# Graph attention plus graph convolution, 64 graphs on one core: key products in two halves, their shared weight tile reloaded in halves, and the key sums taken from the split weights

## The reference, cut to what matters

```python
# x: (64, 256, 512), adj: (64, 256, 256), all float32; LN is a layer norm without gain
h = maximum(LN(x), 0)
query = h @ Wq.T + bq; keyt = h @ Wk.T + bk; value = h @ Wv.T + bv
weight = adj * exp(query @ keyt.T)
weight = weight / sum(weight, axis=2, keepdims=True)
x = x + weight @ value
h = maximum(LN(x), 0)
agg = (adj @ h) / maximum(sum(adj, -1, keepdims=True), 1e-6)
x = x + relu(concatenate([h, agg], 2) @ W.T)
```

## Time and profile before

| | us |
|---|---|
| median of 3 runs | 1933.32 (1931.07 to 1945.87) |
| the profiled execution, its own time | 1942.48 |
| its span | 1940.4 |
| PE busy in it | 1892.7 (98%) |
| DVE busy | 1579.6 (81%) |
| POOL busy | 1103.0 (57%) |
| ACT busy | 862.4 (44%) |
| DMA share of q1 | 57.2% of 16 engines |

### The profile page before, as it was taken

The page is one execution under the profiler, slowest core; times in us unless marked ns, Lnnn a source line. Parts: engine busy times, 40 slices in busy tenths (PEclk is TensorE's granted clock), DMA queues, the critical chain, the costliest instruction groups (busy, mean ns, idle before and its releaser), DMA issues.

```text
span 1940.4 us, 29261 instructions
## 1 busy us (share of the span) xinstructions
PE 1892.7 (98%) x8956; PEld 1576.8 (81%) x8956; DVE 1579.6 (81%) x2649; ACT 862.4 (44%) x1453; POOL 1103.0 (57%) x1066
## 2 busy tenths in 40 slices
PE   8899999999999999999999999999999999999997
PEld 5778888888888888888788888888888888887885
DVE  6887888888788888888878888887888878888776
ACT  4344444444444445443445443444444454434442
POOL 4665565565565565655655655655655656546552
PEclk9999999999999999999999999999999999999999
DMA  6456656566656566555566555566555665555632
GB/s 222 148 189 212 210 181 196 188 203 207 210 178 190 198 205 204 192 198 173 189 208 219 188 194 184 191 211 211 179 191 194 204 203 194 197 173 184 211 125 87
DMA packets 190881, 370.69 MB, mean 191 GB/s; under 512 B 17936, under 2 KB 115216, under 8 KB 182672
## 3 DMA queue, kind: packets, MB, share of 16 engines
q1 hardware_dynamic: 190864, 370.48, 57.2%
HBM read 266.60 MB, written 103.81 MB: 191 GB/s over the span
## 4 chain that ended last, share of the span: by engine, by line
PE 49%; DVE 19%; DMA 17%; issue 8%; SPq 4%; POOL 2%; ACT 1%; DVEq 1%; POOLq 0%; ACTq 0%
PE bank L518 16%; PE bank L520 16%; PE bank L519 16%; DMA turned_store<-blocks 8%; DMA n_l<-t_store 8%; DVE y L1223 3%; SPq L263 3%; DVE x L1235 3%; DVE stats L1091 2%; DVE x L1227 2%; DVE g_full L1213 2%; DVE deg L1112 1%; DVE mean_sum L1096 1%; DVE blocks L1073 1%; DVE sums L1252 1%
## 5 line engine op out<-in xcount | busy, mean ns | idle before, releaser
L403 POOL TENSOR_TENSOR hT_l<-turned,hT_h 128x512 fp32r<-128x512 f32 x122 | 181.9, 1517 | 264.0 <-ACT hT_h L824 263.9
L242 POOL TENSOR_TENSOR w_l<-w,w_h 128x512 fp32r<-128x512 f32 x62 | 80.3, 1295 | 307.5 <-ACT w_h L857 307.5
L1073 DVE STREAM_TRANSPOSE blocks<-h 128x512 f32<-128x512 f32 x252 | 163.3, 685 | 110.3 <-DMA turned_store<-blocks 110.3
L518 PE MATMUL bank<-hT_h,n_h 128*128 128x512 f32 x512 | 200.9, 392 | 3.9 <-DVE hT_l L1164 2.8
L519 PE MATMUL bank<-hT_l,n_h 128*128 128x512 f32 x512 | 200.2, 391 | 0.0
L520 PE MATMUL bank<-hT_h,n_l 128*128 128x512 f32 x512 | 200.2, 391 | 0.0
L518 PE MATMUL bank<-wv_h,hT_h 128*128 128x512 f32 x512 | 199.6, 390 | 0.0
L519 PE MATMUL bank<-wv_l,hT_h 128*128 128x512 f32 x512 | 199.5, 390 | 0.0
L520 PE MATMUL bank<-wv_h,hT_l 128*128 128x512 f32 x512 | 199.3, 389 | 0.0
L399 POOL TENSOR_TENSOR xb<-x_in,bv_b 128x512 f32<-128x512 f32 x128 | 165.9, 1301 | 43.5 <-DVE x L1235 39.3
L843 ACT ACTIVATE kz_h<-bank,kp_bias 128x512 fp32r<-128x512 f32 x128 | 83.6, 675 | 207.5 <-PE bank L520 207.5
(11 more groups left out here) (152 smaller groups left out, 5394.9 us busy)
## 6 DMA issues: line engine op xcount, KB each, us to landing
turned_store<-blocks SPq DMA_DIRECT2D x126, 512.0 KB, 4.5
turned<-turned_store SPq DMA_DIRECT2D x504, 128.0 KB, 2.9
x_in<-x SPq DMA_DIRECT2D x32, 1024.0 KB, 5.3
n_h<-t_store SPq DMA_DIRECT2D x31, 1024.0 KB, 6.3
n_l<-t_store SPq DMA_DIRECT2D x31, 1024.0 KB, 8.3
out<-x SPq DMA_DIRECT2D x124, 256.0 KB, 2.0
n_h<-n_store SPq DMA_DIRECT2D x60, 512.0 KB, 4.6
n_l<-n_store SPq DMA_DIRECT2D x60, 512.0 KB, 5.9
```

The lines of the kernel that those rows point to most:

```text
L242: engine.tensor_tensor(w_l[:, g], w[:, g], w_h[:, g].bitcast(F32), ALU.subtract).then_inc(w_split, 1)
L403: pool.tensor_tensor(by_blocks(hT_l, t), turned_tile(t), by_blocks(hT_h, t).bitcast(F32), ALU.subtract).then_inc(hT_split, 1)
L518: pe.matmul(dst, lh, rh, start=first, stop=False, skip_group_check=more)
L1073: nc.vector.transpose(blocks[:, :, :, t % NT, :].rearrange("p j c b -> p c j b"), h[:, t, :].rearrange("p (c j b) -> p c j b", c=DT, b=Q)) ...
```

## The change

- **Key products in halves.** `kp(i, dt, half)` does two of the four blocks of the inner index. PE does the first halves of all four results, then the second halves. `kp_half` counts the first halves. The waits for the banks of results 2 and 3 (`y_done`, `sum_inv_done`) stay ahead of these results' first halves.
- **T1 and T2 loaded apart.** After `kp_half` SP issues `load_t(0)` (T1, 512 KB high and 512 KB low) ahead of `load_x(i + 1)`; `load_t(1)` (T2) stands where `load_t` stood. `strassen(j, 2)` waits for T1, `strassen(j, 3)` for T2. The n loads have a semaphore for each half.
- **Key sums.** The additions in `split_w`, `high_sum` and `low_sum` are gone, and with them `sum_h` and `sum_l`. `sum_weights` makes four matmuls of 512 columns, from the high and low parts of w's two key tiles. What waited for `sum_split` waits for `w_split`.
- **Order on ACT and DVE in `layer0`.** ACT: two `relu_norm` come ahead of `high_kp(0)`, which is followed by `high_kp(1)`. DVE: `degrees` and `turn_g(j, 0)` come ahead of all four `low_kp`.
- **Setup, first, last and final step.** W1's first half is loaded ahead of x of pair 1, n is stored to DRAM later, and the weight combinations are ordered anew between the engines. In `final_step` DVE does `sum_z` and `low_z` for both rounds, then `combine_s4`, ahead of `degrees`; in `last_step` `layer1_result(j, 3)` comes ahead of `combine_s2(i)`.

```diff
@@ sync
-            def load_t(i):
-                sp.wait_ge(kp_psum, DT * (i + 1))
-                sp.dma_start(n_h[:, :, :].bitcast(F32), t_d[0]).then_inc(t_loaded, 16)
-                sp.dma_start(n_l[:, :, :].bitcast(F32), t_d[1]).then_inc(t_loaded, 16)
+            def load_t(k):
+                half = slice(2 * k, 2 * k + 2)
+                sp.dma_start(n_h[:, half, :].bitcast(F32), t_d[0, :, half, :]).then_inc(t_loaded[k], 16)
+                sp.dma_start(n_l[:, half, :].bitcast(F32), t_d[1, :, half, :]).then_inc(t_loaded[k], 16)
...
             def step(i):
                 j = i - 1
+                sp.wait_ge(kp_half, i + 1)
+                load_t(0)
                 sp.wait_ge(xb_done, T * (i + 1))
                 load_x(i + 1)
                 move_g(j)
-                load_t(i)
+                sp.wait_ge(kp_psum, DT * (i + 1))
+                load_t(1)
@@ split_w
             engine.tensor_tensor(w_l[:, g], w[:, g], w_h[:, g].bitcast(F32), ALU.subtract).then_inc(w_split, 1)
-            engine.wait_ge(w_split, G * i + g + 1)
-            engine.tensor_tensor(w[:, g, 0, :], w[:, g, 0, :], w[:, g, 1, :], ALU.add).then_inc(w_summed, 1)
@@ tensor
             def all_kp(i):
...
-                kp(i, 0)
-                kp(i, 1)
+                kp(i, 0, 0)
+                kp(i, 1, 0)
                 if not is_first(i):
                     pe.wait_ge(y_done, T * (i - 1))
-                kp(i, 2)
+                kp(i, 2, 0)
                 pe.wait_ge(sum_inv_done, i)
-                kp(i, 3)
+                kp(i, 3, 0)
+                if not is_first(i):
+                    pe.wait_ge(n_loaded[1], 32 * (i - 1))
+                for dt in range(DT):
+                    kp(i, dt, 1)
...
-                pe.matmul(every, all_ones, sum_h[:, :, :].rearrange("p g n -> p (g n)"), start=True, stop=False)
-                mm = pe.matmul(every, all_ones, sum_l[:, :, :].rearrange("p g n -> p (g n)"), start=False, stop=True)
+                for n, part in enumerate((w_h, w_l)):
+                    for c in range(NT):
+                        mm = pe.matmul(every, all_ones, part[:, :, c, :], start=(n == 0 and c == 0),
+                                       stop=(n == 1 and c == NT - 1))
@@ scalar, layer0
-                high_kp(i, 0)
                 act.wait_ge(key_bias_done, T * (i + 1))
                 relu_norm(1, src, j, 0)
                 relu_norm(1, src, j, 1)
+                high_kp(i, 0)
                 high_kp(i, 1)
@@ vector, layer0
-                low_kp(i, 0)
                 degrees(j)
-                low_kp(i, 1)
                 dve.wait_ge(h_stored[1], 16 * i)
                 dve.wait_ge(hT_split, T * i)
                 turn_g(j, 0)
-                low_kp(i, 2)
-                low_kp(i, 3)
+                for dt in range(DT):
+                    low_kp(i, dt)
                 turn_g(j, 1)
@@ vector, final_step
-                degrees(j)
                 sum_z(j, 0)
-                low_z(j, 0)
                 sum_z(j, 1)
+                low_z(j, 0)
                 low_z(j, 1)
+                combine_s4(j)
+                degrees(j)
```

More of the change, by code:

```diff
@@ L119, in gnn_layers @@
         adjT = sb("adjT", [P, T, nodes])
-        with nc.sbuf_tensor("z_full", [P, ROUNDS, dim], F32) as z_full:
-            z_sum = (z_full[:, 0], z_full[:, 1])
-        sum_h, sum_l = sb("sum_h", [P, G, nodes], F32R), sb("sum_l", [P, G, nodes], F32R)
+        z_full = sb("z_full", [P, ROUNDS, dim])
+        z_sum = (z_full[:, 0], z_full[:, 1])
         w = sb("w", [P, G, NT, nodes])
@@ L552, in _, with kp @@
             pe.wait_ge(n_split, DT)
-            def kp(i, dt):
+            def kp(i, dt, half):
                 cols = slice(dt * P, (dt + 1) * P)
-                product(bank[KP_BANK[dt]][:, :],
-                        [(n_h[:, c, cols], n_l[:, c, cols], hT_h[:, c, :], hT_l[:, c, :]) for c in range(DT)]
-                        ).then_inc(kp_psum, 1)
+                mm = product(bank[KP_BANK[dt]][:, :],
+                             [(n_h[:, c, cols], n_l[:, c, cols], hT_h[:, c, :], hT_l[:, c, :])
+                              for c in range(2 * half, 2 * half + 2)], start=half == 0, stop=half == 1)
+                if half == 1:
+                    mm.then_inc(kp_psum, 1)
+                elif dt == DT - 1:
+                    mm.then_inc(kp_half, 1)
             def first_kp():
@@ L563, in first_kp @@
                 for dt in range(DT):
-                    kp(0, dt)
+                    for half in range(2):
+                        kp(0, dt, half)
             def all_kp(i):
@@ L919, in first_step @@
                 high_mix(T2)
-                for t in range(NT, T):
+                high_v(0, 2)
+                high_v(0, 3)
+                act.wait_ge(mixed, 4)
+                high_mix(T4)
+                act.wait_ge(v_psum, T)
+                for t in range(T):
                     high_hT(1, t)
@@ L1390, in last_step @@
                 layer1_result(j, 2, LAST_AZ_BANK[2], x1)
+                layer1_result(j, 3, LAST_AZ_BANK[3], x1)
                 combine_s2(i)
-                layer1_result(j, 3, LAST_AZ_BANK[3], x1)
-                combine_s4(i)
             def final_step(i):
                 j = i - 1
+                sum_z(j, 0)
+                sum_z(j, 1)
+                low_z(j, 0)
+                low_z(j, 1)
+                combine_s4(j)
                 degrees(j)
-                sum_z(j, 0)
-                low_z(j, 0)
-                sum_z(j, 1)
-                low_z(j, 1)
                 sum_ha1(j, 0)
```

120 lines of the change are left out of this document (49 added, 71 removed).

## The result

| | kernel before | changed kernel |
|---|---|---|
| median of the timed runs | 1937.06 us (20 runs, 1928.85 to 1945.87) | 1931.32 us (20 runs; 19 of them 1927.84 to 1932.93) |
| profiled execution | 1942.5 us, span 1940.4 | 1931.43 us, span 1929.6 |
| first key product of step 2 | 135.12 us | 132.47 us |
| first key product of step 31 | 1843.21 us | 1836.94 us |
| from there to the end of the span | 97.2 us | 92.7 us |

The ratio of the medians is 0.997, with a 95% interval of 0.9959 to 0.9982 (a disturbed run of 2363 us, among the 20, is left out). So the change gained 0.3%, some 6 us, where 0.8%, 15 us, were forecast: the sign is right, less than half of the size is there. Between the two profiled executions the gain is 1942.5 - 1931.4 = 11.1 us, against 24.6 in the sum of the prediction.

What follows compares the result with a forecast made beforehand. The prediction took PE's matmuls to bound the kernel, with little waiting, mostly for T. Steady part -10.6, beginning -9 and end -5 us gave -24.6 from 1942.5: 1918 us, with an 80% range of 1904 to 1934.

Steps and rivals of the forecast that it cites:

- the wait for T goes: In front of strassen(j, 2): T1 and T2 would land in time, removing 25.2 us of PE waits in steady steps.
- the key sums cost 0.454 us a step: On PE between az and av: two more 512-column matmuls a step, 14.5 us in 32 steps.
- What is late next: Steady waits before strassen(j, 3) and the scores once T is in time: 3.5 us for both together, bounds 1.8 and 9.4.
- The sum for `turn_g(j, 0)`: DVE in step 18: turn_g(j, 0) expected to end at 1085.5 less 0.45 us.
- The third rival: Key products queue behind turn_g(j, 0) on DVE, third low part 1.4 us late each step: 1958 us, chance 0.06.
- the deciding point, 11.5 us: End of turn_g(j, 0) after the first key product, 1085.7 in step 18; if later, PE waits at the scores.
- The second rival: Waits behind take T's place: g tiles no earlier, 12 us of steady waits with S2 late: 1930 us, chance 0.15.
- the range of 80%: Whole kernel: measured time expected between 1904 and 1934 us.
- the forecast's own case: Whole kernel: time between 1910 and 1927 us, chance 0.63.
- The rule that the prediction weighed: Two-SBUF-input DVE instructions and SBUF-reading GpSimd instructions exclude each other; 3 us less POOL work a step would free DVE.
- the beginning, -9 us: Setup and first steps: PE idles and low clock after them shrink, -9 us, bounds -13.8 and -3.
- the end, -5 us: final_step: sum_z right after combine_s2 removes PE's 5.68 us idle before az(j, 0); -5 us, bounds -6.5 and -1.

Runs made afterwards that it cites:

- e6: Kernel before with only T's load split into two pairs with a semaphore each, at the old place, key products whole: 1920.68 us, ratio 0.9893.
- e1: Changed kernel with DVE's old order in layer0 put back, two low parts of the key products ahead of turn_g: 1922.61 us, ratio 0.9916.
- e3: Kernel before with only the key products in halves and T1 loaded between them, all else old: 1919.0 us, ratio 0.9902.
- e2: Changed kernel without the maximum on the degrees, DVE's new order kept: 1927.09 us, ratio 0.9935.
- e7: Changed kernel with DVE's old layer0 order and, in the first step, POOL waiting for w's low parts before its last two weight combinations: 1920.7 us.
- e5: Changed kernel with DVE's old order in layer0 and the old key sums (additions on POOL, two matmuls): 1913.36 us, ratio 0.9855.
- e8: Kernel before with T's load split into two pairs, key products whole, and the new orders of last_step and final_step: 1915.19 us, ratio 0.9865.

## Why the forecast came out too large

**Right: the wait for T goes.** 25.2 us fell to 0.0. T1 is issued at 1078.98 and 1079.38 in step 18, and no landing of n_l in that stretch takes over 6.3 us, so it is there by 1085.7, as expected (before 1086). The reason given was right for T2 too. What the prediction missed is that the halves were not needed for it (e6).

**Right: the key sums cost 0.454 us a step.** The floor of a period went from 57.96 to 58.40. The shift of DVE's chain against PE came as said: the x of the step is done 0.44 us sooner after the first key product than before. But it reached S2 only where DVE's order is the old one (e1).

**Wrong, the step that failed first: "What is late next", the sentence that "the last result is complete at the same time as before. So 0.5 to 3.5 us stay".** The waits at the scores are 12.2 us; with S2 the two places were given 3.5 together and had 14.3, which cost 10.9 by the periods. That is 7.4 us more than forecast; the floor, 58.40 instead of 58.41, gives 0.4 back, and 7.0 us are what the steady part was missed by. The sum for `turn_g(j, 0)` was 1085.5 - 0.45, that is 10.8 us after the first key product; it ended at 11.85. Of the 1.04 us between, 0.68 are the maximum on the degrees, held for 1.02 us instead of the 0.34 that it took in this step before (held there too, but met late in POOL's addition), and 0.34 an idle of DVE ahead of its `layer0`; it stood there before too (0.36) and was left out of the sum. The third rival had this mechanism, its place and the deciding point, 11.5 us, and got 0.06 with a price of 1958 us, because it let `turn_g` keep its whole lateness. What happened is that rival at a quarter of its strength: 0.3 to 0.9 us a step, instead of 1.4. A rival with a threshold isn't an all-or-nothing case. When the forecast lies 0.7 us from the threshold, small stretches decide, and its price grows with the distance past it. e1 takes this away and reaches 1696.2 in the steady part; the prediction had 1697.5.

**The second rival, 1930 us at 0.15, has the measured number, in part by luck.** It put 12 us of waits at `strassen(j, 3)`, where there are 2.1. Its mechanism is there all the same, hidden behind the scores: S2 did not come sooner with the sums and the new order (its low part ends at 35.56 us after the first key product, and at 35.52 in e3, with the old sums), and when the wait at the scores went alone, in e2, S2 cost 6.2 us, where the prediction had 5.9 for an S2 that keeps its place. The first store of g tiles is issued at 11.97 us instead of 12.96 and lands at 17.60 instead of 17.66, behind the 1 MB of x asked for at 10.54; in e1 it is issued at 12.52 and lands at 16.99 (medians of 29 steps). That x's bytes hold this store is read from these times and was not tried. The time lies in the range of 80%, and outside the forecast's own case, which had 0.63.

The rule that the prediction weighed from the Trainium skill, "SBUF — State Buffer", section "Who interferes with whom", was read too narrowly. Beside instructions with two SBUF inputs it also names `tensor_scalar` among the DVE operations that can enter a 2-port mode and then contend with GpSimd, and says that `tensor_reduce` never contends on this chip. The traces agree on each, though none shows an operation's mode: the maximum takes 1.02 us beside the POOL addition and 0.17 apart from it, the reduction 1.20 to 1.22 us in every step, whether POOL's addition covers most of it (e1) or only its end (changed kernel). The prediction looked for the rule's gain, less POOL work, and not for which DVE instruction the new order moves beside which POOL instruction.

**Wrong: the beginning, -9 us, gave -2.65** (bounds -13.8 and -3; it falls just outside, and counted from the first key product of all, 107.0 less 103.8, just inside). The idle ahead of the sums was to go and grew from 1.90 to 3.45 us; the granted clock is low after it in the changed kernel too:

```profile
63.00:66.00 3.00, 3.00 (x9) 2.36 (x9) 3.00 (x5) 0.11 (x1) 3.00 (x3) 0.58 0.95 308
```

That is a window of 63 to 66 us with the columns of the earlier trace rows: PE's clock is at 0.58 after the idle, DVE and POOL are both busy for all of it. The prediction counted the additions that leave DVE, and not that with `low_sum` a wait left POOL behind which the mixes had stood: they now run beside DVE's work on w and hold it for 6.6 us (e7). It named ACT's new order as a risk and gave it no price; e5 shows an idle of 3.60 us behind it. The idle ahead of step 1's key products did go (3.21 to 0.16), and that ahead of its scores fell from 3.95 to 1.66. The 1.69 us for T in step 1 came back at the next place, where PE waits for S2:

```profile
109.84 0.19 PEld L513 LDWEIGHTS bank<-n_h,hT_h 128*128 128x128 f32 x1 [1.47 <-POOL hT_l L411]
```

**Right: the end, -5 us, gave -4.5**, and e8 5.2 by itself. What stays of the idles in `final_step`, with a window at full clock behind them, answers to the earlier trace rows:

```profile
1904.68 0.19 PEld L513 LDWEIGHTS bank<-n_h,hT_h 128*128 128x128 f32 x1 [0.59 <-POOL hT_l L411]
...
1908.09 0.19 PEld L513 LDWEIGHTS bank<-kz_h,at_h 128*128 128x128 f32 x1 [0.82 <-POOL at_l L424]
...
1910.87 0.19 PEld L513 LDWEIGHTS bank<-mix_h,hT_h 128*128 128x128 f32 x1 [1.56 <-ACT g_full L883]
```

```profile
1911.00:1915.00 4.00, 4.00 (x18) 3.31 (x19) 2.03 (x4) 1.50 (x3) 0.68 (x1) 1.00 0.00 0
```

One idle of 5.68 us became three of 0.6 to 1.6, and none of these lowered the clock.

**The parts.** From e3 to e5 the profiled span falls by 5.7 us, 1917.0 to 1911.3: 0.2 before step 2, nothing in the steady part and 5.5 behind it, which is what e8 gains by itself. So the new first step is worth about nothing there. From e5 on, the new sums cost 11.0 us between the spans (9.3 between the medians) and DVE's order 7.3 (8.7). So these two parts of the change cost some 18 us of the 24 that the other two bring (18.1 for the halves, 5.5 for the end). That 1919.0 + 8.7 + 9.3 - 5.5 = 1931.5 meets the measured 1931.3 adds little: e1 and e5 drop out of this sum, and what it tests is that e5, 1913.4, equals e3 less the gain of the end, 1913.5.

**The base.** The sum was made against a profiled execution 9 us above the median shown, and these 9 us were not taken off, on the ground that the wait for T makes up the spread. With 20 runs the median is 1937.1, so the profiled one was 5.4 above it, while the changed kernel's lies on its median. The gain is 11.1 us between profiles and 5.7 between medians. The ground is borne out in part: without the wait for T, 19 runs of the changed kernel lie within 5.1 us, those of the kernel before within 17. But the forecast against the median was 15.3 and against the profile 24.6; taking the smaller for granted hid that the profiled execution lay above most others.

**Open.** Whether the store of the g tiles is held by x's transfer; whether ACT's old order in the first step, together with e7's wait, would shorten the beginning; and how far e5 and e7 add up. None of these was tried.

## What to carry to other kernels

Before halving a computation to hide a load, split the load and its semaphore and wait for each half where it is first read: here that alone brought as much as the halves did. Time an added cost in the kernel that has lost its waits too, since a wait that is left pays for it, and the cost shows up only after the wait is gone. When work or a wait is taken off POOL, ask what POOL then does at that moment, and which short DVE operation now meets it.

## What the hardware showed that was not expected

A maximum over 128 x 4 numbers, `TENSOR_SCALAR` with one SBUF input, takes 0.17 us by itself and up to 1.03 us when it starts inside a POOL addition of 128 x 512. In every such case, 30 steps of the kernel before and 28 of the changed one, it ends 0.02 to 0.03 us after POOL's operation, however early or late it met it. A `RECIPROCAL` of the same 128 x 4 numbers takes 0.18 us and two `STREAM_TRANSPOSE` 1.31 us beside the same addition (e2), as always. Two low parts of w, 128 x 512 each, took 5.66 us on DVE beside POOL operations of 128 x 1024, and 1.29 us with POOL idle; POOL's own operations took 2.73 to 2.85 us in the first case and 2.40 in the second, so both lose, DVE most.

After an idle of 4.11 us in e7 thirteen loads of 512-column matmuls stood 0.43 us apart instead of 0.23, some 2.6 us on top of the idle; after one of 1.56 us at the end of the changed kernel none did. The length of the idle alone doesn't decide it: at the second pair's key products PE idled for 3.21 us in the kernel before and 3.23 in e3, and behind it the granted clock was 0.50 in the first (68.9 to 72 us) and 1.00 in the second (68.1 to 72 us).
